# A three-layer graph network with a mixer and routed experts on one core: one edge tile of every second span fetched row by row

## The reference

```python
def _rgcn_layer(x, W, root, bias, src, dst, seg):
    agg = jax.ops.segment_sum(x[src], seg, num_segments=N_REL * N_NODES)
    agg = agg.reshape(N_REL, N_NODES, -1)
    return jnp.einsum('rnd,rde->ne', agg, W) + x @ root + bias
...
for l in range(N_LAYERS - 1):
    h = jax.nn.relu(_rgcn_layer(h, weights[l], roots[l], biases[l], src, dst, seg))
h = jax.nn.sigmoid(_rgcn_layer(h, weights[-1], roots[-1], biases[-1], src, dst, seg))
...
xn = _layernorm(x, axis=-1)
x = x + gnn(xn) + linear_attention(xn)
x = x + top2_of_8_expert_ffn(_layernorm(x, axis=-1))
```

## Time and profile before

| what | value |
|---|---|
| median of three runs | 3376.06 us |
| the profiled execution's own time | 3373.21 us |
| its span (first to last instruction) | 3371.3 us |
| busy: TensorE | 2836.3 us (84%) |
| busy: GpSimd | 2437.1 us (72%) |
| busy: VectorE | 1177.4 us (35%) |
| busy: ScalarE | 408.3 us (12%) |
| chain that ended last | GpSimd 43%, TensorE 28%, "issue" 19%, DMA 7% |
| mean granted TensorE clock | 0.866 of full speed |

### The profile page before, as it was taken

The page is one execution under the profiler, slowest core; times in us unless marked ns, Lnnn a source line. Parts: engine busy times, 40 slices in busy tenths (PEclk is TensorE's granted clock), DMA queues, the critical chain, the costliest instruction groups (busy, mean ns, idle before and its releaser), DMA issues.

```text
span 3371.3 us, 50935 instructions
## 1 busy us (share of the span) xinstructions
PE 2836.3 (84%) x16420; PEld 2491.9 (74%) x16420; DVE 1177.4 (35%) x2891; ACT 408.3 (12%) x1032; POOL 2437.1 (72%) x2635
## 2 busy tenths in 40 slices
PE   4778778878877888888788887887999999989997
PEld 3677667767776766767677766776888888889896
DVE  5222222222323322222222222334545445545422
ACT  2000000000001000000000000000222222222332
POOL 5777777777776777777777776677777777777343
PEclk8888888888888888777877788777999999999998
DMA  8444444444445333333333334334666666776876
GB/s 201 138 137 137 138 137 138 137 137 137 137 138 169 105 107 107 108 108 107 107 108 108 107 107 129 94 105 135 205 213 222 209 222 218 230 235 223 271 254 227
DMA packets 279171, 527.25 MB, mean 156 GB/s; under 512 B 60927, under 2 KB 182267, under 8 KB 278908
## 3 DMA queue, kind: packets, MB, share of 16 engines
q0 software_dynamic: 121152, 331.40, 33.2%
q1 hardware_dynamic: 156588, 193.06, 17.7%
q10 hardware_dynamic: 1296, 1.24, 0.1%
HBM read 461.33 MB, written 64.17 MB: 156 GB/s over the span
## 4 chain that ended last, share of the span: by engine, by line
POOL 43%; PE 28%; issue 19%; DMA 7%; DVE 1%; ACT 1%; POOLq 0%; SPq 0%; ACTq 0%; DVEq 0%
POOL arena L746 43%; PE bank L1825 6%; DMA arena<-rows_dram,arena 6%; PE bank L1988 5%; PE bank L1984 5%; PE bank L1880 3%; PE bank L1920 2%; PE bank L1930 2%; PE bank L1891 2%; PE bank L1818 1%; PE bank L1816 1%; POOL xs_dram L758 0%; DMA arena<-in_L_mix_b_out_dram 0%; DMA arena<-ys_dram 0%; PE bank L1756 0%
## 5 line engine op out<-in xcount | busy, mean ns | idle before, releaser
L746 POOL DMA_INDIRECT arena<-rows_dram,arena x2396 | 2271.3, 948 | 750.3 <-issue 695.2
L1984 PE MATMUL bank<-arena 128*128 128x128 f32 x4836 | 1062.4, 328 | 454.1 <-DMA arena<-rows_dram,arena 402.6
L1984 PEld LDWEIGHTS bank<-arena 128*128 128x128 f32 x4836 | 838.2, 220 | 654.1 <-DMA arena<-rows_dram,arena 517.3
L1572 DVE TENSOR_TENSOR arena<-arena,bank 128x256 f32 x807 | 338.5, 419 | 1797.8 <-PE bank L1988 1748.3
L1988 PE MATMUL bank<-arena 128*128 128x128 f32 x4836 | 788.5, 307 | 2.8 <-issue 2.8
L1988 PEld LDWEIGHTS bank<-arena 128*128 128x128 f32 x4836 | 719.1, 223 | 1.7 <-issue 1.6
L1825 PE MATMUL bank<-arena 128*128 128x256 f32 x2400 | 602.5, 391 | 3.1 <-DVE zcol L1587 2.9
L1825 PEld LDWEIGHTS bank<-arena 128*128 128x128 f32 x2400 | 446.1, 198 | 52.3 <-issue 3.7
L1491 DVE TENSOR_TENSOR arena<-bank,arena 128x1408 f32<-128x1408 f32 x222 | 355.3, 1603 | 10.0 <-issue 10.0
L1880 PE MATMUL bank<-arena 128*128 128x128 f32 x1216 | 158.5, 287 | 4.0 <-DVE arena L1401 3.7
L1880 PEld LDWEIGHTS bank<-arena 128*128 128x128 f32 x1216 | 153.3, 203 | 5.8 <-issue 4.9
(11 more groups left out here) (249 smaller groups left out, 1501.3 us busy)
## 6 DMA issues: line engine op xcount, KB each, us to landing
arena<-in_L_ffn_W_dram SPq DMA_DIRECT2D x114, 512.0 KB, 4.8
arena<-in_L_ffn_W_dram SPq DMA_DIRECT2D x43, 1024.0 KB, 12.2
arena<-rows_dram,arena POOLq DMA_INDIRECT x2418, 2.7
xs_dram<-zslot SPq DMA_DIRECT2D x25, 1224.0 KB, 6.2
arena<-xs_dram SPq DMA_DIRECT2D x56, 136.0 KB, 4.1
rows_dram<-arena SPq DMA_DIRECT2D x50, 128.0 KB, 3.0
arena<-in_L_gnn_weights_dram SPq DMA_DIRECT2D x6, 1024.0 KB, 10.9
arena<-xs_dram SPq DMA_DIRECT2D x38, 128.0 KB, 2.2
```

The costliest lines, as they stand in the source:

```text
L746: nc.gpsimd.indirect_dma_start(out=gath[:, slot, :], out_offset=None, in_=rows_dram[l], in_offset=bass.IndirectOffsetOnAxis(ap=at[:, slot: ...
L1572: nc.vector.tensor_tensor(acc, acc, edge_sum(l, q).rearrange("p (k r n) -> p k r n", k=KD, r=REL), ALU.add).then_inc(S["tile_add"], 1)
L1984: nc.tensor.matmul(edge_sum(l, q)[:, 0:WC], gath[:, slot, 0:P], onehot[:, slot, :], start=first, stop=last)
```

## The change

In layers 0 and 1 the last tile (slot 32) of every even span of the loop, spans 2, 4, ... 22, is no longer gathered by GpSimd. SyncE loads that tile's 128 row numbers from HBM into one partition (`row_nos`), reads them into registers eight at a time, and issues one DMA of one row (1 KB) for each of partitions 0 to 87. ScalarE does the same for partitions 88 to 127, from the same `row_nos`, in the odd span before, at most two rows at each u. The rows go into a buffer of their own, one per layer (`by_row[l]`), which is free again once the even span before is done; so each tile has the two spans of a pair to arrive in. TensorE waits for 88 and 40 row transfers in place of the slot's gather. GpSimd issues 10 gathers in the last third of these spans.

SyncE's loop changes from one step per store to one step per pair: index load, 5 blocks of 8 rows, store 2i, 6 blocks of 8 rows, store 2i+1. The general path for edges that do not fit the spans gets one more increment and is not run here.

```diff
+ROW_BLOCK, SP_BLOCKS, SP_FIRST = 8, 11, 5
+SP_ROWS = ROW_BLOCK * SP_BLOCKS
+ACT_ROWS = P - SP_ROWS
+BY_ROW = PAIRS
...
+        by_row = [qT[:, NP - D:NP], xrow]
+        row_nos = stats[:, :, :].rearrange("p t n -> p (t n)")[0:1, 0:P].bitcast(I32)
...
+        def takes_rows(l, s):
+            return l < LAYERS - 1 and not isinstance(s.m, int) and s.par == 0
+        def rows_taken(l, i):
+            return BY_ROW * l + i + 1
+        def free_rows(l, i):
+            return GROUPS * l + SG * (2 * i + 1)
+        def edge_rows(l, s, slot):
+            return by_row[l] if slot == SPAN - 1 and takes_rows(l, s) else gath[:, slot, :]
...
-                steps(sp, NT - 1, store)
+                def take(i, b):
+                    _, rows = nc.values_load_multi_w_load_instructions(
+                        row_nos[0:1, ROW_BLOCK * b:ROW_BLOCK * (b + 1)], engines=(sp.engine,), min_val=0, max_val=N_NODES - 1,
...
+                    for j in range(ROW_BLOCK):
+                        p = ROW_BLOCK * b + j
+                        sp.dma_start(by_row[l][p:p + 1, :], rows_dram[l][bass.ds(rows[j], 1), :]).then_inc(S["edge_in"], 16)
+                wait(sp, "rows_st", 16 * (NT - 1) * l)
+                wait(sp, "last_st", 16 * l)
                 sp.wait_ge(S["first_st"], 16 * (NG + LAYERS - 1))
+                with sp.Fori(0, BY_ROW) as i:
+                    sp.wait_ge(S["group_mm"], free_rows(l, i))
+                    sp.nop(nofuse=True)
+                    sp.dma_start(row_nos, src[bass.ds((SPAN * 3 - 1) * P + i * (2 * SPAN * P), P)].rearrange("(o n) -> o n", o=1)).then_inc(S["src_in"], 16)
+                    sp.wait_ge(S["src_in"], 16 * 3 + 16 * rows_taken(l, i))
+                    sp.nop(nofuse=True)
+                    for b in range(SP_FIRST):
+                        take(i, b)
+                    store(2 * i)
+                    for b in range(SP_FIRST, SP_BLOCKS):
+                        take(i, b)
+                    store(2 * i + 1)
+                with sp.Fori(2 * BY_ROW, NT - 1) as t:
+                    store(t)
                 store(NT - 1)
...
-                            for j in range(n):
+                            for j in range(n - 1 if a == CPS - 1 and takes_rows(l, s) else n):
                                 gather(CH * a + j, at)
...
+                        taking = l < LAYERS - 1 and not isinstance(s.m, int) and s.par == 1
+                        if taking:
+                            act.wait_ge(S["group_mm"], free_rows(l, s.i))
+                            wait(act, "last_st", 16 * l)
+                            act.wait_ge(S["src_in"], 16 * 3 + 16 * rows_taken(l, s.i))
+                            act.nop(nofuse=True)
+                            taken = []
                         for u in range(tiles_of(s)):
+                            if taking and u % ROW_BLOCK == 0 and u < 4 * ROW_BLOCK:
+                                at = SP_ROWS + len(taken)
+                                taken += nc.values_load_multi_w_load_instructions(
+                                    row_nos[0:1, at:at + (1 if u else 2) * ROW_BLOCK], engines=(act.engine,), min_val=0, max_val=N_NODES - 1,
...
+                            if taking and u < 4 * ROW_BLOCK:
+                                for j in (2 * u, 2 * u + 1) if u < ROW_BLOCK else (u + ROW_BLOCK,):
+                                    act.dma_start(by_row[l][SP_ROWS + j:SP_ROWS + j + 1, :],
+                                                  rows_dram[l][bass.ds(taken[j], 1), :]).then_inc(S["win_moved"], 16)
...
-                                wait(pe, s_gath[slot], gathered(l, slot, s.m))
+                                if slot == SPAN - 1 and takes_rows(l, s):
+                                    pe.wait_ge(S["edge_in"], 16 * 6 + 16 * SP_ROWS * rows_taken(l, s.i))
+                                    pe.wait_ge(S["win_moved"], 16 * 2 + 16 * ACT_ROWS * rows_taken(l, s.i))
+                                else:
+                                    wait(pe, s_gath[slot], gathered(l, s, slot))
...
-                                nc.tensor.matmul(edge_sum(l, q)[:, 0:WC], gath[:, slot, 0:P], onehot[:, slot, :], start=first, stop=last)
+                                nc.tensor.matmul(edge_sum(l, q)[:, 0:WC], edge_rows(l, s, slot)[:, 0:P], onehot[:, slot, :], start=first, stop=last)
```

More of the change, by code:

```diff
@@ L81 @@
 PIECE_CALLS = ((), (0, 1, 2), (3, 4, 5), (6, 7, 8), (9, 10, 11), (12, 13, 14, 15))
+ROW_BLOCK, SP_BLOCKS, SP_FIRST = 8, 11, 5
+SP_ROWS = ROW_BLOCK * SP_BLOCKS
+ACT_ROWS = P - SP_ROWS
+BY_ROW = PAIRS
+assert ACT_ROWS == 5 * ROW_BLOCK and SP_ROWS * 16 * BY_ROW * (LAYERS - 1) < 1 << 15
 GE = GT * P
@@ L484, in fills, with gathered @@
             return (CHUNKS + 1 - h) // 2 - (1 if (CHUNKS - 1) % 2 == h and j >= LAST_CHUNK else 0)
-        def gathered(l, slot, m):
+        def takes_rows(l, s):
[6 more added lines that the diff above has]
+            return by_row[l] if slot == SPAN - 1 and takes_rows(l, s) else gath[:, slot, :]
+        def gathered(l, s, slot):
+            m = s.m
+            if slot == SPAN - 1:
+                each = NSPAN - 1 - BY_ROW
+                if l == LAYERS - 1:
+                    return (each * l + m + 1) * 16
+                return (each * l + (1 if is_first(s) else s.i + 2)) * 16
             return ((NSPAN if slot < LAST_SPAN else NSPAN - 1) * l + m + 1) * 16
@@ L567, in store @@
                         sp.dma_start(xs_tiles[:, bass.ds(t * ZERO_T, ZERO_T), :], zeros(ZERO_T)).then_inc(S["zero_st"], 16)
-                steps(sp, NT - 1, store)
-                sp.wait_ge(S["first_st"], 16 * (NG + LAYERS - 1))
+                def take(i, b):
+                    _, rows = nc.values_load_multi_w_load_instructions(
+                        row_nos[0:1, ROW_BLOCK * b:ROW_BLOCK * (b + 1)], engines=(sp.engine,), min_val=0, max_val=N_NODES - 1,
+                        skip_runtime_bounds_check_because="an edge's source is a node, as for the gathers")
+                    for j in range(ROW_BLOCK):
[3 more added lines that the diff above has]
+                wait(sp, "last_st", 16 * l)
+                sp.wait_ge(S["first_st"], 16 * (NG + LAYERS - 1))
+                with sp.Fori(0, BY_ROW) as i:
[12 more added lines that the diff above has]
+                    store(t)
                 store(NT - 1)
@@ L796, in span @@
                                 wait_apart(pool, "ring_made", rings(l, s))
-                            for j in range(n):
+                            for j in range(n - 1 if a == CPS - 1 and takes_rows(l, s) else n):
                                 gather(CH * a + j, at)
                                 if j in REST_AFTER:
-                                    wait_apart(pool, s_gath[CH * a + j - 1], gathered(l, CH * a + j - 1, s.m))
+                                    wait_apart(pool, s_gath[CH * a + j - 1], gathered(l, s, CH * a + j - 1))
                         if final and not (is_int(s.m, 0) or is_int(s.m, 1)):
@@ L1029, in span @@
                             mix_exp()
-                        for u in range(tiles_of(s)):
+                        taking = l < LAYERS - 1 and not isinstance(s.m, int) and s.par == 1
[5 more added lines that the diff above has]
+                            taken = []
+                        for u in range(tiles_of(s)):
+                            if taking and u % ROW_BLOCK == 0 and u < 4 * ROW_BLOCK:
+                                at = SP_ROWS + len(taken)
+                                taken += nc.values_load_multi_w_load_instructions(
+                                    row_nos[0:1, at:at + (1 if u else 2) * ROW_BLOCK], engines=(act.engine,), min_val=0, max_val=N_NODES - 1,
+                                    skip_runtime_bounds_check_because="an edge's source is a node, as for the gathers")[1]
+                            if taking and u < 4 * ROW_BLOCK:
+                                for j in (2 * u, 2 * u + 1) if u < ROW_BLOCK else (u + ROW_BLOCK,):
+                                    act.dma_start(by_row[l][SP_ROWS + j:SP_ROWS + j + 1, :],
+                                                  rows_dram[l][bass.ds(taken[j], 1), :]).then_inc(S["win_moved"], 16)
                             if not is_first(s):
@@ L1983, in span @@
                                     nc.tensor.matmul(edge_sum(l, q)[:, 0:WC], hn[0:LAST, 0:P], missed[0:LAST, q * WC:(q + 1) * WC], start=False, stop=False)
-                                nc.tensor.matmul(edge_sum(l, q)[:, 0:WC], gath[:, slot, 0:P], onehot[:, slot, :], start=first, stop=last)
+                                nc.tensor.matmul(edge_sum(l, q)[:, 0:WC], edge_rows(l, s, slot)[:, 0:P], onehot[:, slot, :], start=first, stop=last)
                                 if last:
                                     for v in range(GT * q, u + 1):
-                                        mm = nc.tensor.matmul(edge_sum(l, q)[:, WC:2 * WC], gath[:, v, P:2 * P], onehot[:, v, :],
```

(2 more changed lines are left out.)

## The result

The changed kernel takes 3345.02 us (median of 4 runs, 3341.61 to 3352.47), the kernel before 3373.60 us on the same chip (4 runs, 3370.99 to 3379.72): a ratio of 0.992 with a 95% interval of 0.9907 to 0.9933. That is 28.6 us less, where 27.5 were forecast. Run again later, the change gave 0.9903 (0.9888 to 0.9917). The profiled execution has a span of 3343.3 us against 3371.3.

The account below looks back on a forecast made before the run. GpSimd's gathers, one per 1.25 us, were taken to bound layers 0 and 1. 22 fewer save 27.5 us, other terms cost nothing: from the 3376.06 us median to 3348.6 us, range shown 3342 to 3366 us.

Parts of the forecast that it names:

- The bound and the main term: GpSimd's gathers set the time in layers 0 and 1; 22 fewer at a 1.25 us beat save 27.5 us.
- SyncE's 88 rows: SyncE, per pair of spans: 0.45 us per row, 68.3 us with loads and stores out of 81.5, so hidden.
- The load of eight numbers: SyncE's register load of eight row numbers: taken as 2.2 us, between bounds of 0.27 and 2.61 us.
- the late-rows rival: SyncE's pair exceeds 81.5 us, TensorE waits at tile 32; decides from 0.57 us per row; about 4320 us; chance 0.09.
- every excess counts in full: SyncE starts the next pair only after TensorE's wait at tile 32, so lateness is paid in full, 22 times.
- the sign that the prediction gave for being wrong: TensorE waiting at the first matmul of tile 32 for `rows_dram` rows from SyncE's queue would show the forecast wrong.
- the chance of 0.09: Probability given to the slower outcome, rows arriving late on SyncE and a kernel of about 4320 us.
- 40 rows cost nothing: ScalarE, odd span: 0.39 us per row; mixer's copy about 1 us late in layer 0, within 8.3 us of slack.
- The load of sixteen: ScalarE's register load of 16 row numbers: priced at 4.0 us by the slope of TensorE's loads.
- One DMA engine: All 128 rows may share one of 16 DMA engines; crowding would give back the gain, about 3376 us; chance 0.06.
- 61 ns per packet: Packet time on SyncE's queue, called a sixth of the 0.35 us or so per row at which one engine crowds.

Follow-up runs that it names:

- e7: The change with a second gather per even span left out too (44 in all) and no rows fetched, slot 30 multiplied instead: 3320.14 us, ratio 0.9845.
- e1: The change with its 22 gathers still left out but no rows fetched, TensorE multiplying slot 31 for slot 32: 3354.71 us, ratio 0.9922.
- e2: The change with all gathers back and used, the rows still fetched and waited for but unused: 3373.72 us, ratio 0.9979 to the kernel before.
- e3: The change with SyncE fetching all 128 rows of the tile and ScalarE none: 3343.1 us, ratio 0.9888 to the kernel before.
- e6: The change with SyncE fetching each of its 88 rows three times, TensorE waiting for all: 3990.31 us, ratio 1.1825 to the kernel before.
- e4: The change with SyncE fetching each of its 88 rows twice, TensorE waiting for both: 3375.67 us, ratio 0.9985 to the kernel before.
- e9: The change with two tiles by rows in layer 1 (SyncE 160 rows, ScalarE 96), one by SyncE in layer 0: 3392.26 us, ratio 1.0046.
- e11: As e9, but in layer 1 SyncE fetches 144 rows and ScalarE 112: 3332.15 us, ratio 0.9863 to the kernel before.
- e5: The change with two tiles per even span by rows, 128 by SyncE and 128 by ScalarE: 3536.31 us, ratio 1.0481 to the kernel before.

## Why the prediction was right, point by point

*The bound and the main term.* Right. 22 gathers at a beat of 1.25 us were to give 27.5 us; the pairs of layer 1 shrank by 1.25 us, those of layer 0 by 1.07. e7 nearly repeats it with 22 more, and e1 and e2 show that the gathers alone make the difference. The missing 0.18 us per pair of layer 0 (2 us) was not in the sum. Without rows it is 0.10 (e1), with all rows on SyncE 0.04 (e3), so the rows are not shown to be its cause, and the cause stays open.

*SyncE's 88 rows.* The step was mis-sized, on the safe side. I took 0.45 us per row; rows follow each other at 0.41 us. A one-row DMA takes 0.23 us on the queue where the 128-row load of the earlier trace rows took 0.33, and the gaps around it are longer than the 0.05 us that I took. The load of eight numbers, which I interpolated at 2.2 us from TensorE's queue, takes 0.78 us on SyncE: the nearest row was one of another engine, and the row of SyncE's own one-number load (0.27 us) would have been nearer. In all 52 us per pair in place of 67.

The prediction set this against the Trainium skill (DMA: Bandwidth & Descriptors, Rules for kernel authors), which advises against many small transfers. By its fixed 2.0 us per DMA (Anatomy of one DMA; the Trainium skill gives it there for transfers that GpSimd issues), paid in series, the 264 DMAs of a pair in e6 would have taken 528 us, an estimate. The pair there was 109.3 us, so in this case the measurement decides: the fixed part of one transfer runs beside the next, and only the issue adds up.

*The threshold of the late-rows rival.* The bound was right, the sign was wrong. The prediction put the limit where the last row lands near 80 us after the pair's start, and said that "every excess counts in full" beyond it. e4 stands on both sides: with the last row issued some 77.5 us after the index load nothing to speak of is lost (layer 1), with 80 us the pairs go to 85.4 (layer 0), though only after TensorE's slack has taken up some 10 us, which the prediction left out. In terms of SyncE's cycle, from one index load over the rows, their landing and TensorE's passing tile 32 to the next: where it is longer than GpSimd's pair it sets the pair, 86.3 against 80.3 us in e9, about 109 against 81.5 in e6; where it is not, the rows cost nothing, 78.25 in e11 against 80.45. What does not tell is the sign that the prediction gave for being wrong, TensorE waiting at tile 32 for rows from SyncE: e4 has that in every pair of layer 1, 7.5 us a time, at 0.19 us per pair. For the change itself the cycle had some 25 us to spare, so the chance of 0.09 was, on these rows, too high.

*ScalarE.* Right that 40 rows cost nothing (e3). The load of sixteen was priced 4.0 us and took at most 1.2. That rows ahead of ScalarE's copies can cost TensorE more than its slack is shown by e5, at 128 rows.

*One DMA engine.* The packet count was confirmed. The prediction set 61 ns per packet against 0.35 us per row and called it a sixth; a row is two packets, 122 ns, so it was a third. Crowding was not seen in the change, in e2 or in e6: gathers land as before in the first two, and with 304 rows per pair in e6 SyncE's DMAs still took 0.22 us each at the median. Only e4 has longer landings, in layer 0 above all, and there the cause is open. Which of the 16 engines the rows use, the trace does not tell.

*The size of the agreement.* Luck in part: 28.6 against 27.5 us hides a loss of 2 us in layer 0's loop and a gain of about 3 outside the loops that other profiles of the same code give or take.

## What to carry to other kernels

When one engine works at a fixed beat and nothing it waits for is late, every instruction taken off it is worth nearly its whole beat, gap included, and the same work on idle queues may be much dearer (some 71 us of SyncE for a tile in e3 against 1.25) and still be free. Its limit is then not the work but the closed cycle of the helper: from its start over the landing and the consumer's release to its next start; as long as that cycle is no longer than the bound engine's own, a late arrival is paid from the consumer's slack, and a wait of the consumer is no sign of loss by itself. Helper instructions on an engine that also does work for the critical consumer had better go behind that work in program order, as e5 and layer 1 of e11 suggest.

## What the runs showed that I had not expected

A DMA of one row of 1 KB occupies SyncE's queue for 0.23 us, one of 128 rows for 0.33 us. A register load costs 0.27 us for one number, 0.78 for eight and 1.23 for sixteen on SyncE, while TensorE took 1.03 us for three: a price read on one engine did not hold for another. And 5.8 us of difference between two profiles, in stretches that the change does not touch, is ordinary here; a cadence that repeats, 11 pairs to a layer, resolves about 0.1 us where the total resolves several.
